# GNN on one core: first columns of edges counted beside the second table's zeroing, and the lower triangle in f32

## The chip, the cores and the metric

The kernel runs on one core of a Trainium2 chip. The metric is the device time of one execution, in microseconds. The median of three runs of the kernel before is 6590.73 us (6584.82 to 6592.37).

## The reference

Four graph layers follow each other on 3125 nodes with 96 features and 103125 directed edges (50000 random pairs in both directions, and one loop per node):

```
x = LN(x + GAT(x, edges))        # 3 layers, 4 heads: softmax over each node's edges
x = LN(x + GIN(x, src, dst))     # segment_sum(x[src], dst), then an MLP with batch norm
x = LN(x + dot_attention(x))     # softmax over edges of q[src].k[dst]
x = LN(x + edge_MLP(x, edge_attr_32))
```

An edge can occur more than once. The first three layers need for each pair of nodes only how often the pair is an edge. So the kernel counts the edges into a dense table of 3200 x 3200 cells once, and computes the layers densely from it.

## The kernel before, in words

`program` (line 101) calls `begin`, then `make_tables`, three attention layers, the other layers, and a store. Each part is a block of instructions per engine, and the next part starts when the last engine has finished the one before. The change is all in `begin` (line 175), the first stage.

`begin` does several things side by side. SyncE (SP) loads the inputs, and then issues the writes that zero the two halves of the count table in device memory (lines 241 to 245): two u16 tables `counts[0]` and `counts[1]` of 3200 x 3200 cells, each zeroed by 16 transfers from a tile of zeros, a row of 10,000 bytes from every partition, and by one small transfer of two bytes per partition, for 128 spare cells. All of these raise one semaphore, `zeroed`. Behind them on the same queue go 52 transfers that clear the table of sorted edges (line 250), whose rows are 16 x 34 x 4 = 2176 bytes a partition. TensorE and ScalarE project the first attention layer.

The edges lie in 806 columns of 128 (`ET` = 806), in 62 groups of `G` = 13 columns. For each group VectorE's `count(g)` (lines 385 to 406) finds, in every column, the edges that name the same cell. TensorE copies each column's cell numbers along the free axis into PSUM (line 331). VectorE compares them with the column itself into `same` (line 390), waits until the adds of the group before last have landed (lines 396 and 397), because `cell_slot` and `cell_add` have two halves only, sums `same` (398), casts the sums to `cell_add` (399), multiplies `same` by the lower triangle `earlier` (400), sums again (401), and so finds which edge is the first of its cell. The others are sent to a spare cell (402 to 405). Then `slots_ready` rises. `same` and `earlier` are bf16.

GpSimd (POOL) adds the counts into the table, one column with one indirect DMA (line 315, the "add" from here on): 128 read-modify-writes of two bytes each in device memory. It reads `cell_slot` and `cell_add`, which VectorE wrote. Two adds into one table may not be in flight together, since one that reads a cell before the other has written it would lose a count. So column t goes into table t % 2 and waits until the add before it in that table, t - 2, has landed. Before column 0 POOL waits for `zeroed`, 16 x 2 x 17, that is for both tables (line 308). At the end it waits for the last adds (line 318), and the block ends.

Beside the groups VectorE and TensorE find where each edge belongs in the sorted order: `members` after group 5 (line 417 is its long comparison), a histogram, and `place` after groups 16 to 36 (lines 455 to 460).

Of the kernel before, what the change touches and what calls it, by code (L numbers as in the profile page):

```python
# [19 lines left out]
P = 128  # L20
NT = -(-N // P)
NP = NT * P
NFULL = N // P
NREST = N - NFULL * P
ET = -(-E // P)
EREST = E - (P - 1) * ET
G = 13
# [30 lines left out]
f32, bf16, i32, u16 = mybir.dt.float32, mybir.dt.bfloat16, mybir.dt.int32, mybir.dt.uint16  # L58
ALU = mybir.AluOpType
# [4 lines left out]
def bcast_rows(ap, n):  # L64

    return ap.unsqueeze(0).to_broadcast([n, ap.shape[0]])
# [34 lines left out]
def program(nc, a, out):  # L101
    ctx = ExitStack()
    with ctx:
# [14 lines left out]
        with ExitStack() as c2:  # L118
# [14 lines left out]
            def project_first(xT, block, entry):  # L133
# [7 lines left out]
                return psum_free  # L141

            begin(nc, a, x, ident, wext, arow, counts, edges, project_first)
            make_tables(nc, a, ident, halves_rows, log_counts, edges)

# [22 lines left out]
def load_gat_weights(sp, a, layer, wext, arow, loaded):  # L168

    sp.dma_start(wext[:, 0:D], a["L0_gnn_W"][layer]).then_inc(loaded, 16)  # L170
    for k, name in enumerate(("L0_gnn_att_src", "L0_gnn_att_dst")):
        sp.dma_start(arow[:, k, :], bcast_rows(a[name][layer].rearrange("h c -> (h c)"), D)).then_inc(loaded, 16)


def begin(nc, a, x, ident, wext, arow, counts, edges, project):
# [6 lines left out]
    with ctx:  # L182
        ctx.enter_context(nc.cleanup_on_exit())
        sb = lambda n, s, d=f32: ctx.enter_context(nc.sbuf_tensor("pl" + n, s, d))
        sem = lambda n: nc.alloc_semaphore("st" + n)
        zeros = sb("zeros", [P, ZF], u16)
# [1 line left out]
        src_i, dst_i, block_i, local_i, part_i = (sb(n, [P, ET], i32) for n in ("src_i", "dst_i", "block_i", "local_i", "part_i"))  # L188
        cell, block_f, slot_f = (sb(n, [P, ET]) for n in ("cell", "block_f", "slot_f"))
        ends = sb("ends", [P, ET, 2])  # L190
        earlier, before, ones = (sb(n, [P, P], bf16) for n in ("earlier", "before", "ones"))
        xT = sb("xT", [D, NP])

        cell_slot = sb("cell_slot", [P, 2, G], i32)
        cell_add = sb("cell_add", [P, 2, G], u16)
# [18 lines left out]

        zeros_set, padded, x_padded, loaded, const_made, consts_ready, steps, row_cleared, row_made, rows_cleared = (
            sem(n) for n in ("zeros_set", "padded", "x_padded", "loaded", "const_made", "consts_ready", "steps", "row_cleared", "row_made", "rows_cleared"))
        zeroed = sem("zeroed")
        cells_made, slots_ready, rows_ready, rows_free = (sem(n) for n in ("cells_made", "slots_ready", "rows_ready", "rows_free"))
        added = [sem(f"added{w}") for w in range(2)]
        members_made, counted, hist_kept, summed, base_made, base_stored, rank_ready, rank_used, slots_made, stored = (  # L220
# [3 lines left out]
        HALF_T = RANK_T // 2  # L224
        LOADS = 11
        ZEROS = NP * NP // (P * ZF)
        with nc.Block() as block:
            @block.sync
            def _(sp):
                load_gat_weights(sp, a, 0, wext, arow, loaded)  # L230
                sp.wait_ge(x_padded, 1)
                sp.dma_start(x[:, 0:NFULL, :], a["x"][0:NFULL * P, :].rearrange("(t p) d -> p t d", p=P)).then_inc(loaded, 16)
                sp.dma_start(x[0:NREST, NFULL, :], a["x"][NFULL * P:N, :]).then_inc(loaded, 16)

                sp.wait_ge(padded, 2)
                for ap, t in ((a["src"], src_i), (a["dst"], dst_i)):
                    for lo, hi in ((0, 112), (112, P - 1)):
                        sp.dma_start(t[lo:hi, :], ap[lo * ET:hi * ET].rearrange("(p t) -> p t", t=ET)).then_inc(loaded, 16)
                    sp.dma_start(t[P - 1:P, 0:EREST], ap[(P - 1) * ET:E].rearrange("(p t) -> p t", p=1)).then_inc(loaded, 16)
                sp.wait_ge(zeros_set, 1)  # L240
                for part in counts:
                    v = part[0:NP * NP, :].rearrange("(p j f) o -> j p (f o)", p=P, f=ZF)
                    for j in range(ZEROS):
                        sp.dma_start(v[j], zeros[:]).then_inc(zeroed, 16)
                    sp.dma_start(part[NP * NP:NP * NP + P, :], zeros[:, 0:1]).then_inc(zeroed, 16)

                sp.wait_ge(row_made, 1)
                sorted_groups = edges["sorted"][:, :].rearrange("(g p k) w -> g p (k w)", p=P, k=TB)
                for g in range(SORTED_GROUPS):
                    sp.dma_start(sorted_groups[g], unused_row[:].rearrange("p k w -> p (k w)")).then_inc(rows_cleared, 16)  # L250

                sp.wait_ge(base_made, 1)
                sp.dma_start(edges["base"][:, :].rearrange("(c p) b -> p c b", p=P), base[:]).then_inc(base_stored, 16)
                sp.wait_ge(base_stored, 16)
                for n, (t, m) in enumerate(pieces):
                    if n >= 2:
                        sp.wait_ge(rank_used, n - 1)
                    sp.dma_start(base_row[:, n % 2, 0:m, :].rearrange("p t b -> p (t b)"),
                                 bcast_rows(edges["base"][t:t + m, :].rearrange("t b -> (t b)"), P)).then_inc(row_loaded[n % 2], 16)
                sp.wait_ge(base_made, 2)  # L260
                sp.dma_start(edges["column"][:, :].rearrange("(p c) o -> p (c o)", p=P), column_i[:]).then_inc(stored, 16)
                sp.wait_ge(slots_made, 1)
                sp.dma_start(edges["ends"][:, :, :], ends[:]).then_inc(stored, 16)
                sp.dma_start(edges["slot"][:, :], block_i[:]).then_inc(stored, 16)
                sp.wait_ge(stored, 48)
                sp.wait_ge(rows_cleared, 16 * SORTED_GROUPS)
# [38 lines left out]

            @block.gpsimd
            def _(pool):
                pool.wait_ge(zeroed, 16 * len(counts) * (ZEROS + 1))
                for t in range(ET):
                    g, j = divmod(t, G)  # L310
                    if j == 0:
                        pool.wait_ge(slots_ready, g + 1)
                    if t >= 2:
                        pool.wait_ge(added[t % 2], 16 * (t // 2))
                    nc.gpsimd.indirect_dma_start(counts[t % 2][:, :], bass.IndirectOffsetOnAxis(ap=cell_slot[:, g % 2, j:j + 1], axis=0),  # L315
                                                 cell_add[:, g % 2, j:j + 1], None, compute_op=ALU.add).then_inc(added[t % 2], 16)
                for w in range(2):
                    pool.wait_ge(added[w], 16 * (ET // 2))

            @block.tensor  # L320
            def _(pe):
# [53 lines left out]
            def _(dve):  # L375
# [9 lines left out]
                def count(g):  # L385

                    half = g % 2
                    key = cell[:, g * G:(g + 1) * G]
                    dve.wait_ge(rows_ready, g + 1)
                    nc.vector.tensor_tensor(same[:], rows[:, 0:G * P].rearrange("p (t c) -> p t c", c=P),  # L390
                                            key.unsqueeze(2).to_broadcast([P, G, P]), ALU.is_equal).then_inc(rows_free, 1)
                    dve.wait_ge(rows_free, g + 1)
                    if g >= 2:

                        done = (g - 1) * G
                        dve.wait_ge(added[0], 16 * -(-done // 2))
                        dve.wait_ge(added[1], 16 * (done // 2))
                    step(nc.vector.reduce_sum(nlow[:], same[:], axis=AX.X))  # L398
                    step(nc.vector.tensor_copy(cell_add[:, half, :], nlow[:]))
                    step(nc.vector.tensor_tensor(same[:], same[:], earlier[:].unsqueeze(1).to_broadcast([P, G, P]), ALU.mult))  # L400
                    step(nc.vector.reduce_sum(nlow[:], same[:], axis=AX.X))
                    step(nc.vector.tensor_scalar(first[:], nlow[:], 0.0, None, ALU.is_equal))
                    step(nc.vector.tensor_scalar(moved[:], key, spare[:, 0:1], None, ALU.subtract))
                    step(nc.vector.tensor_tensor(moved[:], moved[:], first[:], ALU.mult))
                    step(nc.vector.tensor_scalar(cell_slot[:, half, :], moved[:], spare[:, 0:1], None, ALU.add))
                    dve.sem_inc(slots_ready, 1)
# [1298 lines left out]
```

## Time and profile before

| | us |
|---|---|
| median of 3 runs | 6590.73 |
| lowest, highest | 6584.82, 6592.37 |
| the profiled execution, first to last instruction | 6972.0 |
| add (line 315), 806 of them, busy | 1310.8 |
| idle of POOL just before them | 430.7 |
| first and last start of an add | 138.0, 1742.7 |

For the profiled execution nothing but this span is given. "Busy" is the time in which an engine worked on instructions; "idle before" is the time between the end of its previous instruction and the start of this one, with the one who ended most of it. Of an add the time is that which POOL takes to make its descriptors, not the transfer, which lands later.

### The profile page before, as it was taken

To read this page: it belongs to the slowest core of one execution; us is meant where nothing else is said; L and a number is where in the kernel's file an instruction comes from. 1 tells how busy PE (TensorE), PEld (TensorE's weight loads), DVE (VectorE), ACT (ScalarE), POOL (GpSimd) and SP (SyncE) were. 2 spreads that over 40 slices of the span, in tenths; PEclk is the share of its full clock that TensorE was granted. 3 is DMA by queue.
4 is the path that set the end of the run, shared out by engine and by line. 5 is a ranking of instruction groups with operands and counts; after the bars stand their busy time and mean duration, and the time that the engine had idled before them with its cause. 6 is when DMAs were issued, how large, how long until landed. Compare 5 with 4: busy or idle time off the path is not lost. (4 is left out here: it accounts for less than half of the span.)

```text
span 6972.0 us, 62328 instructions
## 1 busy us (share of the span) xinstructions
PE 3698.9 (53%) x21452; PEld 2183.6 (31%) x21452; DVE 3889.8 (56%) x4318; ACT 2472.8 (35%) x4050; POOL 4020.6 (58%) x3151
## 2 busy tenths in 40 slices
PE   2111111110428888477784878876888454555444
PEld 1111011110424444244442444443333232333232
DVE  1434443332679996599965999654999521121113
ACT  1000000000327777377773777721666311111111
POOL 1888878888607667076670666701860256655652
PEclk6555555555668898698985889877888666665656
DMA  9222222222979987398962898752222111111111
GB/s 330 1 7 18 18 18 7 0 0 0 327 235 209 205 208 149 88 212 200 209 147 78 206 208 206 157 181 90 82 77 72 32 39 41 43 41 40 41 39 24
DMA packets 410083, 747.21 MB, mean 107 GB/s; under 512 B 173421, under 2 KB 251291, under 8 KB 405678
## 3 DMA queue, kind: packets, MB, share of 16 engines
q0 software_dynamic: 237024, 305.69, 28.3%
q1 hardware_dynamic: 169534, 436.30, 18.7%
q8 instruction: 178, 2.92, 0.2%
q10 hardware_dynamic: 3216, 1.23, 0.1%
q14 instruction: 131, 1.07, 0.0%
HBM read 628.59 MB, written 114.40 MB: 107 GB/s over the span
## 5 line engine op out<-in xcount | busy, mean ns | idle before, releaser
L315 POOL DMA_INDIRECT counts<-plcell_add,plcell_slot x806 | 1310.8, 1626 | 430.7 <-issue 236.9
L1574 POOL DMA_INDIRECT emxg<-xtab,emsrc x832 | 804.7, 967 | 555.5 <-DVE emsrc L1616 299.6
L398 DVE TENSOR_REDUCE plnlow<-plsame 128x13 f32<-128x1664 bf16 x62 | 117.0, 1888 | 1032.7 <-DMA counts<-plcell_add,plcell_slot 1032.6
L331 PE MATMUL plrows<-ident,plcell 128*128 128x128 f32 x806 | 186.0, 421 | 943.6 <-DVE plsame L390 942.9
L1659 PE MATMUL emps_m<-emwe,emfeatT 128*128 128x384 f32 x416 | 280.6, 769 | 682.4 <-issue 367.1
L652 ACT ACT_TABLE_LOAD x1 | 1.3, 1283 | 1706.5 <-PE mtps L640 1706.5
L1626 DVE TENSOR_TENSOR emsame<-emlocal_id,emrow 128x512 f32<-128x512 f32 x208 | 144.4, 694 | 694.8 <-DMA plbase_row<-slot_base 495.8
L1086 PE MATMUL ga1psE<-ident,ga1logit 128*128 128x128 f32 x2500 | 404.0, 301 | 228.8 <-DMA ga1logit<-log_counts 146.4
L1086 PE MATMUL ga2psE<-ident,ga2logit 128*128 128x128 f32 x2500 | 405.6, 303 | 222.1 <-DMA ga2logit<-log_counts 145.8
L1086 PE MATMUL ga0psE<-ident,ga0logit 128*128 128x128 f32 x2500 | 406.9, 303 | 219.1 <-DMA ga0logit<-log_counts 151.4
L1598 ACT ACTIVATE emfeatT<-emps_f 128x128 f32<-128x128 f32 x208 | 57.8, 278 | 1199.6 <-remote 740.0
L331 PEld LDWEIGHTS plrows<-ident,plcell 128*128 128x128 f32 x806 | 161.4, 224 | 976.8 <-DVE plsame L390 975.9
L1040 ACT ACTIVATE ga1prob<-ga1psE,ga1src_fifth 128x512 f32<-128x512 f32 (+1 forms) x700 | 405.4, 667 | 153.6 <-PE ga1psE L1086 130.5
L1040 ACT ACTIVATE ga2prob<-ga2psE,ga2src_fifth 128x512 f32<-128x512 f32 (+1 forms) x700 | 405.0, 665 | 152.0 <-PE ga2psE L1086 123.6
L1040 ACT ACTIVATE ga0prob<-ga0psE,ga0src_fifth 128x512 f32<-128x512 f32 (+1 forms) x700 | 405.6, 669 | 139.4 <-PE ga0psE L1086 124.9
L1086 PEld LDWEIGHTS ga2psE<-ident,ga2logit 128*128 128x128 f32 x2500 | 293.7, 151 | 448.1 <-issue 265.1
L1086 PEld LDWEIGHTS ga0psE<-ident,ga0logit 128*128 128x128 f32 x2500 | 293.8, 151 | 447.0 <-issue 252.9
L1086 PEld LDWEIGHTS ga1psE<-ident,ga1logit 128*128 128x128 f32 x2500 | 291.3, 150 | 453.0 <-issue 280.2
L1668 PE MATMUL emps_a<-emmsg,emsame 128*128 128x96 f32 x1664 | 387.5, 375 | 22.8 <-DVE emsame L1626 8.5
L1668 PEld LDWEIGHTS emps_a<-emmsg,emsame 128*128 128x128 f32 x1664 | 338.0, 271 | 196.0 <-issue 195.1
L1470 ACT ACTIVATE dotwork<-dotpsS 128x640 f32<-128x640 f32 x500 | 313.1, 708 | 205.9 <-PE dotpsS L1418 204.5
L1502 DVE TENSOR_TENSOR dotwork<-dotwork,dotcnt 128x1280 f32<-128x1280 f32 x250 | 374.8, 1499 | 8.6
(339 smaller groups left out, 9058.8 us busy)
## 6 DMA issues: line engine op xcount, KB each, us to landing
ga0logit<-log_counts POOLq DMA_DIRECT2D x96, 512.0 KB
ga1logit<-log_counts POOLq DMA_DIRECT2D x96, 512.0 KB
ga2logit<-log_counts POOLq DMA_DIRECT2D x96, 512.0 KB
counts<-plzeros SPq DMA_DIRECT2D x32, 1250.0 KB
mthalf<-counts SPq DMA_DIRECT2D x50, 800.0 KB
log_counts<-mtlogs SPq DMA_DIRECT2D x25, 1600.0 KB
ga0near<-log_counts SPq DMA_DIRECT2D x50, 800.0 KB
ga1near<-log_counts SPq DMA_DIRECT2D x50, 800.0 KB
```

The lines of the kernel that those rows point to most:

```text
L315: nc.gpsimd.indirect_dma_start(counts[t % 2][:, :], bass.IndirectOffsetOnAxis(ap=cell_slot[:, g % 2, j:j + 1], axis=0), cell_add[:, g % 2, ...
L331: last = nc.tensor.transpose(rows[:, j * P:(j + 1) * P], cell[:, g * G + j:g * G + j + 1].to_broadcast([P, P]), ident[:])
L398: step(nc.vector.reduce_sum(nlow[:], same[:], axis=AX.X))
L1040: nc.scalar.activation(prob[:, u % P_BUFS, 0:width], psE[:, u % E_BUFS, 0:width], ACT.Exp, bias=src_fifth[:, tile(r, t), h:h + 1]).then_in ...
L1086: last = nc.tensor.transpose(psE[:, u % E_BUFS, q * P:(q + 1) * P], logit[:, r % L_BUFS, q, t * P:(t + 1) * P], ident[:])
L1470: nc.scalar.activation(work[:, t % W_BUFS, 2 * g:2 * g + 2, f * HW:(f + 1) * HW], psS[:, n % S_BUFS, :, 0:HW], ACT.Exp).then_inc(exp_ready, 1)
L1502: nc.vector.tensor_tensor(w, w, cnt[:, t % C_BUFS, cols].unsqueeze(1).to_broadcast([P, HEADS, HW]), ALU.mult).then_inc(prob_ready, 1)
L1574: nc.gpsimd.indirect_dma_start(xg[:, h, t, :], None, xtab[:, :], bass.IndirectOffsetOnAxis(ap=src[:, h, t:t + 1], axis=0)).then_inc(gather ...
L1598: nc.scalar.activation(featT[:, v % 2, :], ps_f[:, 0:P], ACT.Copy).then_inc(feat_kept, 1)
L1626: nc.vector.tensor_tensor(same[:, v % 2, :, :], local_id[:].unsqueeze(1).to_broadcast([P, CT, P]), row[:, g % ROWS, lo:lo + CT, ED:ED + 1] ...
L1659: nc.tensor.matmul(ps_m[:, v % 2, 0:CT * D], featT[:, v % 2, :], we[:].rearrange("p t d -> p (t d)"), start=True, stop=True).then_inc(pre_ ...
L1668: last = nc.tensor.matmul(flat_a[:, bass.ds(lo, D)], same[:, w % 2, t, :], msg[:, w % 2, t, :], start=False, stop=(w == CHUNKS - 1 and t = ...
```

## The change

Each table gets its own semaphore, `zeroed[0]` and `zeroed[1]`. POOL waits for the one at the first add into its table. The first 16 columns (`LONE`) all go into table 0, each waiting for the one before; column 16 is the first of table 1, and from there columns alternate. `table_of(t)` gives the table and how many adds it has had; `adds_before(t, w)` counts those of the columns before t, for VectorE's wait and for the one at the end. `earlier` becomes f32; `same` stays bf16.

```diff
-        earlier, before, ones = (sb(n, [P, P], bf16) for n in ("earlier", "before", "ones"))
+        earlier = sb("earlier", [P, P])
+        before, ones = (sb(n, [P, P], bf16) for n in ("before", "ones"))
...
-        zeroed = sem("zeroed")
+        zeroed = [sem(f"zeroed{w}") for w in range(2)]
...
+        LONE = 16
+
+        def table_of(t):
+
+            return (0, t) if t < LONE else ((t - LONE + 1) % 2, LONE + (t - LONE) // 2 if (t - LONE) % 2 else (t - LONE) // 2)
+
+        def adds_before(t, w):
+
+            return sum(table_of(u)[0] == w for u in range(t))
...
-                for part in counts:
+                for part, done in zip(counts, zeroed):
...
-                        sp.dma_start(v[j], zeros[:]).then_inc(zeroed, 16)
-                    sp.dma_start(part[NP * NP:NP * NP + P, :], zeros[:, 0:1]).then_inc(zeroed, 16)
+                        sp.dma_start(v[j], zeros[:]).then_inc(done, 16)
+                    sp.dma_start(part[NP * NP:NP * NP + P, :], zeros[:, 0:1]).then_inc(done, 16)
...
-                pool.wait_ge(zeroed, 16 * len(counts) * (ZEROS + 1))
                 for t in range(ET):
                     g, j = divmod(t, G)
+                    w, n = table_of(t)
                     if j == 0:
                         pool.wait_ge(slots_ready, g + 1)
-                    if t >= 2:
-                        pool.wait_ge(added[t % 2], 16 * (t // 2))
-                    nc.gpsimd.indirect_dma_start(counts[t % 2][:, :], bass.IndirectOffsetOnAxis(ap=cell_slot[:, g % 2, j:j + 1], axis=0),
-                                                 cell_add[:, g % 2, j:j + 1], None, compute_op=ALU.add).then_inc(added[t % 2], 16)
+                    if n == 0:
+                        pool.wait_ge(zeroed[w], 16 * (ZEROS + 1))
+                    else:
+                        pool.wait_ge(added[w], 16 * n)
+                    nc.gpsimd.indirect_dma_start(counts[w][:, :], bass.IndirectOffsetOnAxis(ap=cell_slot[:, g % 2, j:j + 1], axis=0),
+                                                 cell_add[:, g % 2, j:j + 1], None, compute_op=ALU.add).then_inc(added[w], 16)
                 for w in range(2):
-                    pool.wait_ge(added[w], 16 * (ET // 2))
+                    pool.wait_ge(added[w], 16 * adds_before(ET, w))
...
-                        done = (g - 1) * G
-                        dve.wait_ge(added[0], 16 * -(-done // 2))
-                        dve.wait_ge(added[1], 16 * (done // 2))
+                        for w in range(2):
+                            if adds_before((g - 1) * G, w):
+                                dve.wait_ge(added[w], 16 * adds_before((g - 1) * G, w))
```

## Rows read from the trace of the kernel before

**Rows 1.** The page, 40 slices of the span: busy tenths of POOL.
```profile
POOL 1888878888607667076670666701860256655652
```

**Rows 2.** The page's groups: busy, mean ns | idle before and who ended it.
```profile
L315 POOL DMA_INDIRECT counts<-plcell_add,plcell_slot x806 | 1310.8, 1626 | 430.7 <-issue 236.9
...
L398 DVE TENSOR_REDUCE plnlow<-plsame 128x13 f32<-128x1664 bf16 x62 | 117.0, 1888 | 1032.7 <-DMA counts<-plcell_add,plcell_slot 1032.6
```

**Rows 3.** Line 315: durations in ns (min/median/max), first and last start in us.
```profile
L315 POOL DMA_INDIRECT counts<-plcell_add,plcell_slot x806: 1557/1561/21401, 138.0 to 1742.7; - x162
```

**Rows 4.** Timeline, group 2: start us, us, instruction [idle before <-releaser].
```profile
180.05 1.89 DVE L398 TENSOR_REDUCE plnlow<-plsame 128x13 f32<-128x1664 bf16 x1 [104.99 <-DMA counts<-plcell_add,plcell_slot]
...
182.19 1.02 DVE L400 TENSOR_TENSOR plsame<-plsame,plearlier 128x1664 bf16<-128x1664 bf16 x1
182.47 2.18 POOL L315 DMA_INDIRECT counts<-plcell_add,plcell_slot  x1 [0.30 <-issue]
...
184.95 1.56 POOL L315 DMA_INDIRECT counts<-plcell_add,plcell_slot  x1 [0.30 <-issue]
```

**Rows 5.** Timeline, group 61, the last.
```profile
1698.90 1.02 DVE L400 TENSOR_TENSOR plsame<-plsame,plearlier 128x1664 bf16<-128x1664 bf16 x1
1699.12 2.24 POOL L315 DMA_INDIRECT counts<-plcell_add,plcell_slot  x1 [0.30 <-issue]
```

**Rows 6.** Timeline, `members` after group 5.
```profile
265.06 21.15 DVE L417 TENSOR_TENSOR plmember<-plblock_f,plblock_id 128x20150 bf16<-128x20150 f32 x1
266.23 21.40 POOL L315 DMA_INDIRECT counts<-plcell_add,plcell_slot  x1 [0.30 <-issue]
```

**Rows 7.** Timeline, a much later stage, gathers beside a comparison in f32.
```profile
5614.95 0.69 DVE L1626 TENSOR_TENSOR emsame<-emlocal_id,emrow 128x512 f32<-128x512 f32 x1 [0.22 <-PE emps_a L1668]
5615.00 1.46 POOL L1574 DMA_INDIRECT emxg<-xtab,emsrc  x1 [3.48 <-DVE emsrc L1616]
5616.76 0.95 POOL L1574 DMA_INDIRECT emxg<-xtab,emsrc  x1 [0.31 <-issue]
```

**Rows 8.** Timeline, the first comparison of group 3, one operand in PSUM.
```profile
186.24 1.89 DVE L390 TENSOR_TENSOR plsame<-plrows,plcell 128x1664 bf16<-128x1664 f32 x1
186.82 1.56 POOL L315 DMA_INDIRECT counts<-plcell_add,plcell_slot  x1 [0.30 <-issue]
```

**Rows 9.** Groups by line and form, DVE, 150 to 1744 us: busy, mean ns | idle.
```profile
L390 DVE TENSOR_TENSOR plsame<-plrows,plcell 128x1664 bf16<-128x1664 f32 x59 | 111.5, 1891 | 5.7
L400 DVE TENSOR_TENSOR plsame<-plsame,plearlier 128x1664 bf16<-128x1664 bf16 x60 | 61.5, 1025 | 2.1
...
L459 DVE TENSOR_TENSOR plranked<-plranked,plmember 128x1000 f32<-128x1000 f32 x20 | 24.0, 1200 | 0.7
```

**Rows 10.** Timeline of DVE: the slots of group 1 are ready.
```profile
72.79 0.23 DVE L405 TENSOR_SCALAR plcell_slot<-plmoved,plspare 128x13 int32<-128x13 f32 x1
```

**Rows 11.** Timeline of SP's DMA queue: start us, us that the issue took.
```profile
60.77 15.71 SPq L244 DMA_DIRECT2D counts<-plzeros  x1
...
98.26 68.04 SPq L250 DMA_DIRECT2D sorted_edges<-plunused_row  x52
```

**Rows 12.** Three stretches: length, busy of five engines, PEclk, DMA share, GB/s.
```profile
20.00:60.00 40.00, 36.40 (x128) 22.27 (x127) 10.44 (x38) 15.00 (x28) 0.00 (x0) 0.83 1.01 421
60.00:65.00 5.00, 1.23 (x6) 0.82 (x4) 4.68 (x8) 0.00 (x0) 0.00 (x0) 0.50 1.66 118
120.00:125.00 5.00, 0.00 (x0) 0.00 (x0) 0.00 (x0) 0.00 (x0) 0.00 (x0) 0.50 1.73 217
```

**Rows 13.** Timeline of POOL: adds 0, 4, 6 and 12.
```profile
137.97 1.79 POOL L315 DMA_INDIRECT counts<-plcell_add,plcell_slot  x1 [135.18 <-DMA counts<-plzeros]
...
151.77 1.56 POOL L315 DMA_INDIRECT counts<-plcell_add,plcell_slot  x1 [3.15 <-DMA counts<-plcell_add,plcell_slot]
...
158.62 1.56 POOL L315 DMA_INDIRECT counts<-plcell_add,plcell_slot  x1 [3.18 <-DMA counts<-plcell_add,plcell_slot]
...
176.88 1.56 POOL L315 DMA_INDIRECT counts<-plcell_add,plcell_slot  x1 [1.12 <-DMA counts<-plcell_add,plcell_slot]
```

## The prediction, made before the changed kernel was run

> **What bounds the kernel now.** I read the slices first. POOL is nearly idle in the first slice and at 70 to 80% in the next nine, which is the first stage [rows 1]. The groups say with what: 806 adds, busy for 1310.8 us, with 430.7 us idle before them, of which 236.9 is issue, that is POOL's own 0.30 us between two adds [rows 2]. VectorE waits in that stage: before line 398 it idles 1032.7 us in total, until adds land [rows 2]; less the 105.0 us of group 2 [rows 4] that is 15.7 us for each of the 59 groups behind it. So POOL's chain of adds, from 138.0 to 1742.7 us [rows 3], is the stage, and the later stages start when it is done. What lengthens one add, or moves the first, moves the end; VectorE has some 15 us a group to spare. The pace is 1.56 + 0.30 = 1.86 us an add.
>
> The timeline then shows that adds are not all alike. In group 2 one add takes 2.18 us in place of 1.56; it starts 0.28 us after VectorE began line 400, and ends 1.44 us after line 400's end, where 1.56 less about 0.12 would put an add that had stood still until then [rows 4]. In the last group it is the same: 2.24 us, started 0.22 us in [rows 5]. Following the timeline, each of the 60 groups between has one add that starts in line 400's 1.02 us, 0.22 to 0.79 us after its start. The totals confirm it: 1310.8 less 806 x 1.561 [rows 3] is 52.6 us; one long add took 21.40 - 1.56 = 19.8 of it [rows 6]; 32.8 us is left, or 0.55 us in each of 60 groups.
>
> **The triangle in f32.** Two questions: how long is line 400 then, and does an add still stand still behind it.
>
> Duration. Line 400 has bf16 throughout and takes 1.025 us. Line 390 has as many elements with f32 among its inputs and takes 1.891 us; line 459 multiplies f32 by bf16, 1000 elements, in 1.200 us, the same rate for its size [rows 9]. So I take 1.89 us, 0.866 us more. Bounds: 0 (1.025 us stays) and 0.87.
>
> The standing still. It does with f32 inputs and at the slow rate: line 417 runs 21.15 us, an add that starts 1.17 us into it takes 21.40 us, so it resumed when line 417 was over [rows 6]. It does with f32 inputs and an f32 output: line 1626 runs 0.69 us, a gather that starts 0.05 us into it takes 1.46 us, the next 0.95 [rows 7]. What does not do it is one SBUF operand: line 390, with one operand in PSUM, runs for 1.89 us and the add that starts inside takes 1.56 [rows 8]. So it is not the bf16 rate that holds POOL, but two operands in SBUF, and line 400 keeps both there. The add that starts 0.3 us in will stand until 1.89 instead of 1.02. The next one would start after that, so one add a group is hit as now.
>
> Cost: 60 x 0.866 = 52.0 us, all on POOL's chain, which has no slack inside a group. Bounds: if in an execution without the profiler the adds fall otherwise against line 400, the added stall of a group is anything from 0 (no start in the longer window) to 0.87; 0 and 52 us. I take 52, since the only trace there is shows the hit in all 60 groups. VectorE's own chain grows by 0.87 us a group, under those 15.7 us.
>
> The Trainium skill ("SBUF — State Buffer", Who interferes with whom) says that a VectorE instruction with two SBUF inputs contends with a GpSimd instruction that reads SBUF, whatever the mode; the trace agrees, 19.8 us in [rows 6] and none in [rows 8]. The same section infers that a tensor_tensor should leave descriptor generation alone, as it takes only the read side; by that the whole term would be nothing, and [rows 4, 6] speak against it, the index columns being read from SBUF.
>
> **The first adds.** The slots of groups 0 and 1 are ready at 73.0 us [rows 10]. When is table 0 zeroed? The rate drops from 421 GB/s to a mean of 118 in 60 to 65 us and 217 in 120 to 125 [rows 12]: it stops at 60 + 5 x 118/421 = 61.4 us and at 122.6 us, where each table's bulk is out and its small transfer waits for it. After the second stop, POOL goes 15.4 us later, at 137.97 [rows 13]. SP's issue of a transfer at 60.77 is held for 15.71 us, to 76.5 [rows 11]. Both give 76.5 to 76.8 us for table 0. The first add starts at 76.8, 61.2 us sooner.
>
> Each of the 16 must then land before the next starts. Undisturbed, add 12 starts at 176.88 and VectorE, which waits for it, goes at 180.05 [rows 13, 4]: 3.2 us from one to the next. Beside the clearing of sorted edges it is 158.62 - 151.77 = 6.85 us [rows 13]. Beside the zeroing no row shows it. Bounds: 3.2 us, and an add that does not land before 138. The pieces there are 10,000 bytes against 2,176, and the small transfer needed 15.4 us to land behind such pieces. The extra 3.65 us behind small pieces, times 4.6, would make 20 us an add; I take the 15.4 that was seen.
>
> Now: 61.2/15.4 = 4.0 adds by 138; to 177, where clearing ends, 39/6.85 = 5.7 more; the other 6.3 at 3.2 us take 20 us. Add 16 starts at 197; before, at 184.95 [rows 4]. So this part costs 12 us: before, the twelve adds up to 176.88 went two in flight, one in each table, and this order gives that up exactly where landing is slow. At the ends: with 3.2 us all 16 are done by 128, add 16 waits for table 1 until 138, and from there everything runs as before but 16 adds ahead, 16 x 1.86 = 30 us gained. With none done by 138, 5.7 come by 177 and 10.3 x 3.2 = 33 us more, 210 us, a loss of 25. With the clearing's 6.85 us it would be a gain of 4.
>
> The Trainium skill ("DMA: Bandwidth & Descriptors", Queues, rings and completion order) says that a completion increment lands only after every earlier write of that DMA engine, across its queues; the wait of 15.4 us in [rows 12, 13] agrees. By this rule an add beside the zeroing waits for the zero pieces in front of it.
>
> **At nothing.** One more wait at column 16 (both adds and zeroes done by then); the f32 memset and select of `earlier`, before 3 us, under POOL's idle 135 us; queue order of SP's transfers, unchanged; the counts of the two tables, whose sum alone is used later. Group 2's slots need 13 landed adds, and 13 more adds of group 1 cover them.
>
> **Sum.** Against the profiled execution: 6972.0 + 52 + 12 = 7036 us. The runs' median lies 381 us below its span, and I can't say in which stage; I carry the difference over as it is: 6590.7 + 64 = 6655 us.
>
> **Rivals.** (a) The f32 triangle frees POOL: line 400 leaves the fast bf16 rate and with it whatever held the adds. This ends on the other side: the 0.55 us of each group goes, 60 x 0.55 = 33 us gained, and with the loss of 12 the time is 6570 us; it decides wherever one add starts inside line 400. For it: the only bf16 product is the one that stalls adds in every group. Against it: [rows 6, 7], which are clear. 3%.
>
> (b) The early adds do overlap the zeroing: they land in 3.2 us, 30 us are gained, 6590.7 + 52 - 30 = 6613 us. For it: an add moves 128 x 2 bytes. Against: 6.85 us behind much smaller pieces. 15%.
>
> (c) The stall does not grow by all of 0.87 us a group, since without the profiler adds and line 400 stand otherwise: halfway, 26 us, 6590.7 + 26 + 12 = 6629 us; at its end, 6603. For it: the profiled execution is 5.8% longer, so something in it is slower. Against: adds and line 400 are tied, VectorE starting on the landing of an add. 15%.
>
> (d) The adds also hold up the zeroing behind them, as the small transfer did for 15.4 us: with three such stops table 1 and the clearing are 46 us late, and the lone adds stay slow longer: 6590.7 + 52 + 12 + 46 = 6701 us at most. Against: POOL's adds between 138 and 177 went beside the clearing with no stop of that length. 5%.
>
> The forecast has 62%, its own range 6635 to 6668 us (the stall at 45 to 52, the start at 0 to 25). The range reaches down to (b) and (c): 6605 to 6675. No change that a measurement can tell is within 0.2%, 13 us: 6577.5 to 6604; there lie the far end of (c) and (b) with part of (c), 6%. Faster has (a) and (b) with all of (c), 5%. Slower 89%.
>
> **What would show it.** Line 400 at 1.89 us, and one add a group near 3.0 us (2.18 + 0.87); the adds' mean at 1.69 us, 1363 us busy. If those adds are at 1.56 us, (a) is right. First add near 77 us; gaps of about 13 us between the next few, and add 16 near 197 us. If add 16 stands at 138 us, (b) is right. The last add near 1807 us; everything behind it shifted and otherwise as it was. Wrong would be a line 400 at 1.02 us, or a stage that ends with other than POOL.

## The result, and the profile after

The changed kernel takes 6638.31 us (median of four runs; 6632.37 to 6639.27), the kernel before on the same chip 6587.77 us (also four runs). The ratio is 1.008, with a 95% interval of 1.0067 to 1.0092: 50.5 us slower, where 64 us were forecast, and the time lies inside the range.

Start with the adds on POOL. These are the page's groups and the view of line 328 (the old 315) of the changed kernel; the columns are those of [rows 2, 3]. The lone line behind them is that of the kernel before.

```profile
L328 POOL DMA_INDIRECT counts<-plcell_add,plcell_slot x806 | 1360.0, 1687 | 433.8 <-issue 235.1
...
L411 DVE TENSOR_REDUCE plnlow<-plsame 128x13 f32<-128x1664 bf16 x62 | 117.0, 1888 | 1035.6 <-DMA counts<-plcell_add,plcell_slot 1035.6
```

```profile
L328 POOL DMA_INDIRECT counts<-plcell_add,plcell_slot x806: 1557/1562/21399, 78.4 to 1795.1; - x162
its engine sat idle before it (us, times) until:
  issue: 235.1, 761
  DMA counts<-plcell_add,plcell_slot: 123.2, 44
  DMA counts<-plzeros: 75.6, 1
```

```profile
  DMA counts<-plcell_add,plcell_slot: 58.6, 40
```

The last add starts at 1795.1 us; before, at 1742.7 [rows 3]. The 52.4 us split into two parts: the adds are busy 1360.0 - 1310.8 = 49.2 us longer, and POOL idles 433.8 - 430.7 = 3.1 us longer before them [rows 2]. The first add is 59.6 us sooner, but the waits for landings grow from 58.6 to 123.2 us, which takes all of it back.

Next, where the 49 us are. The groups of VectorE (150 to 1800 us, columns as in [rows 9]), and the timeline of groups 3 and 61, answering to [rows 4, 5]:

```profile
L413 DVE TENSOR_TENSOR plsame<-plsame,plearlier 128x1664 bf16<-128x1664 bf16 x60 | 113.5, 1892 | 2.1
```

```profile
213.25 1.89 DVE L413 TENSOR_TENSOR plsame<-plsame,plearlier 128x1664 bf16<-128x1664 bf16 x1
213.71 2.86 POOL L328 DMA_INDIRECT counts<-plcell_add,plcell_slot  x1 [0.30 <-issue]
...
1750.31 1.89 DVE L413 TENSOR_TENSOR plsame<-plsame,plearlier 128x1664 bf16<-128x1664 bf16 x1
1750.83 2.81 POOL L328 DMA_INDIRECT counts<-plcell_add,plcell_slot  x1 [0.30 <-issue]
```

The multiply takes 1.892 us in place of 1.025. (The view names the first input's type, bf16; the triangle's f32 doesn't show in it, the duration does.) In each of the 59 groups from 3 on one add starts inside it, 0.21 to 0.98 us after its start, and ends 1.4 us after its end; most take 3.0 us where they took 2.16. VectorE's idle time before line 411 is 1035.6 us, against 1032.7 [rows 2]: the longer multiply takes nothing from VectorE's spare time, and the stage is longer because POOL's adds are.

Last, the start of the stage, answering to [rows 13]. The timeline of POOL: adds 0, 1, 4, 5, 6, then 15 and 16.

```profile
78.35 1.79 POOL L328 DMA_INDIRECT counts<-plcell_add,plcell_slot  x1 [75.57 <-DMA counts<-plzeros]
87.31 1.59 POOL L328 DMA_INDIRECT counts<-plcell_add,plcell_slot  x1 [7.17 <-DMA counts<-plcell_add,plcell_slot]
...
114.66 1.56 POOL L328 DMA_INDIRECT counts<-plcell_add,plcell_slot  x1 [7.64 <-DMA counts<-plcell_add,plcell_slot]
125.69 1.56 POOL L328 DMA_INDIRECT counts<-plcell_add,plcell_slot  x1 [9.47 <-DMA counts<-plcell_add,plcell_slot]
141.93 1.56 POOL L328 DMA_INDIRECT counts<-plcell_add,plcell_slot  x1 [14.68 <-DMA counts<-plcell_add,plcell_slot]
...
189.38 1.56 POOL L328 DMA_INDIRECT counts<-plcell_add,plcell_slot  x1 [1.82 <-DMA counts<-plcell_add,plcell_slot]
191.25 1.56 POOL L328 DMA_INDIRECT counts<-plcell_add,plcell_slot  x1 [0.30 <-issue]
```

Beside the zeroing one lone add follows the other after 9.0 us, and add 5, whose landing meets the stretch in which table 1's small transfer is under way, takes 16.2 us. Add 16 starts at 191.25; before, at 184.95 [rows 4]. The early start bought nothing: add 16 is 6.3 us behind.

The profiled execution spans 6636.3 us, while that of before spanned 6972.0 for a kernel that runs in 6588. The edit doesn't explain that difference: GpSimd's first transfer of the second stage still starts 52 us later than before (1802.3 against 1750.0), while the edge layer's gathers ran from 5515.1 to 6862.7 us before and from 5502.4 to 6546.4 us after, 304 us less, with nothing edited there. So only the first stage is compared between those two traces.

### The profile page after: what moved, and what is told of

The parts are those of the page before. It is cut to its first block and busy times, and to the rows that moved or that the text cites. A ratio compares the mean times of both kernels' runs of the same rounds, so it can differ in the third digit from the quotient of the medians.

```text
span 6636.3 us, 62328 instructions
## 1 busy us (share of the span) xinstructions
PE 3847.1 (58%) x21452; PEld 2266.4 (34%) x21452; DVE 3921.9 (59%) x4318; ACT 2493.0 (38%) x4050; POOL 4053.6 (61%) x3151
## 5 line engine op out<-in xcount | busy, mean ns | idle before, releaser
L328 POOL DMA_INDIRECT counts<-plcell_add,plcell_slot x806 | 1360.0, 1687 | 433.8 <-issue 235.1
L411 DVE TENSOR_REDUCE plnlow<-plsame 128x13 f32<-128x1664 bf16 x62 | 117.0, 1888 | 1035.6 <-DMA counts<-plcell_add,plcell_slot 1035.6
L1643 DVE TENSOR_TENSOR emmsg<-emps_m,emxg 128x384 f32<-128x384 f32 x208 | 115.9, 557 | 812.4 <-DMA emxg<-xtab,emsrc 791.8
L1681 PE MATMUL emps_a<-emmsg,emsame 128*128 128x96 f32 x1664 | 455.8, 453 | 147.9 <-DVE emsame L1639 135.2
L1681 PEld LDWEIGHTS emps_a<-emmsg,emsame 128*128 128x128 f32 x1664 | 404.5, 311 | 381.7 <-issue 377.9
L1672 PE MATMUL emps_m<-emwe,emfeatT 128*128 128x384 f32 x416 | 340.2, 921 | 76.2 <-ACT emfeatT L1611 76.2
L941 DVE CUSTOM_DVE_ANT_0 ga1unused<-ga1near,src_row 128x1600 bf16<-128x1600 f32 x200 | 366.2, 1831 | 8.2 <-DMA ga1near<-log_counts 6.0
```

The costliest lines, as they stand in the source:

```text
L328: nc.gpsimd.indirect_dma_start(counts[w][:, :], bass.IndirectOffsetOnAxis(ap=cell_slot[:, g % 2, j:j + 1], axis=0), cell_add[:, g % 2, j:j ...
L941: nc.vector.tensor_tensor_reduce(out=unused[:], in0=near[:, f, :], in1=src_row[:, h, f * HALF:(f + 1) * HALF], scale=1.0, scalar=LOWEST, o ...
L1643: nc.vector.tensor_tensor(msg[:, v % 2, :, :].rearrange("p t d -> p (t d)"), ps_m[:, v % 2, 0:CT * D], xg[:, g % 2, lo:lo + CT, :].rearran ...
L1672: nc.tensor.matmul(ps_m[:, v % 2, 0:CT * D], featT[:, v % 2, :], we[:].rearrange("p t d -> p (t d)"), start=True, stop=True).then_inc(pre_ ...
L1681: last = nc.tensor.matmul(flat_a[:, bass.ds(lo, D)], same[:, w % 2, t, :], msg[:, w % 2, t, :], start=False, stop=(w == CHUNKS - 1 and t = ...
```

## Experiments

The first four ran beside 21 runs of the kernel before (median 6583.86 us), the last four beside another 21 (6594.10 us). A difference in us is one of medians; the ratio, with its 95% interval, is worked out from all runs, and the two can differ by some 3 us.

**The triangle alone.** Lines of the kernel before, with this edit:

```diff
-        earlier, before, ones = (sb(n, [P, P], bf16) for n in ("earlier", "before", "ones"))
+        earlier = sb("earlier", [P, P])
+        before, ones = (sb(n, [P, P], bf16) for n in ("before", "ones"))
```

> The kernel before with the lower triangle in f32 and nothing else. Theory (two SBUF operands hold POOL for as long as the VectorE instruction runs): line 400 takes 1.89 us, one add a group takes about 3.0 us instead of 2.15, 60 x 0.85 = 51 us more. Rival 1 (the f32 triangle costs little and the 50 us came from the first adds): within 10 us of before. Rival 2 (only the bf16 rate holds POOL): 33 us less than before.

Measured: 6635.38 us, ratio 1.0077 (1.0063 to 1.0090), 51.5 us slower. The page's row of the adds:

```profile
L316 POOL DMA_INDIRECT counts<-plcell_add,plcell_slot x806 | 1363.1, 1691 | 431.3 <-issue 237.0
```

Busy 52.3 us longer, idle as before. This is the theory's number, in runs and in the trace, and both rivals fall. The triangle alone costs as much as the whole change did in its first measurement.

**The lone columns alone.** The changed kernel with the first edit above taken back.

> The changed kernel with the triangle back in bf16: the first 16 columns go into table 0 alone. Theory: add 16 starts 6 us later than in the kernel before, as in the changed kernel, so 6 us more than before (0 to 12). Rival 1 (the first adds made the 50 us): 50 us more. Rival 2 (the overlap does gain what it was to gain, and the triangle hid it): 20 to 30 us less.

Measured: 6592.59 us, ratio 1.0010 (1.0001 to 1.0019), 8.7 us more. Both rivals fall: neither 50 us more nor 20 to 30 less is near it. The adds' row: busy as before, idle 8.9 us longer.

```profile
L327 POOL DMA_INDIRECT counts<-plcell_add,plcell_slot x806 | 1309.9, 1625 | 439.6 <-issue 234.8
```

**The f32 triangle, read from PSUM.** TensorE copies it once with the identity; the prefix sums move into the histogram's bank, so that a bank is free. The f32 lines of the first experiment belong to this edit too; they, the new semaphore and VectorE's one wait for it are left out here.

```diff
-            psB = ctx.enter_context(nc.psum_tensor("plpsB", [P, 512], f32))
+            psE = ctx.enter_context(nc.psum_tensor("plpsE", [P, 512], f32))
+            psB = psH[:, 256:512]
...
                 psum_free(pe)
+                nc.tensor.matmul(psE[:, 0:P], ident[:], earlier[:], start=True, stop=True).then_inc(triangle_made, 1)
...
-                    step(nc.vector.tensor_tensor(same[:], same[:], earlier[:].unsqueeze(1).to_broadcast([P, G, P]), ALU.mult))
+                    step(nc.vector.tensor_tensor(same[:], same[:], psE[:, 0:P].unsqueeze(1).to_broadcast([P, G, P]), ALU.mult))
```

> The kernel before with the triangle in f32, copied once by TensorE into a PSUM bank of its own and read from there by line 400 (the prefix sums share the histogram's bank). The multiply still runs at the slow rate, but has one SBUF operand. Theory (two SBUF operands hold POOL): line 400 at 1.9 us, no add stretched by it, so the 0.55 us of each group goes too: 33 us less than before. Rival (a longer line 400 holds POOL longer, wherever its operands lie): 50 us more, as with the f32 triangle in SBUF.

Measured: 6549.20 us, ratio 0.9943 (0.9929 to 0.9957), 34.7 us less than before. The adds' row on the page, the multiply's group, and the timeline of group 2:

```profile
L318 POOL DMA_INDIRECT counts<-plcell_add,plcell_slot x806 | 1278.0, 1586 | 428.9 <-issue 235.0
```

```profile
L405 DVE TENSOR_TENSOR plsame<-plsame,plpsE 128x1664 bf16<-128x1664 bf16 x60 | 113.3, 1888 | 2.1
```

```profile
184.02 1.89 DVE L405 TENSOR_TENSOR plsame<-plsame,plpsE 128x1664 bf16<-128x1664 bf16 x1
184.32 1.56 POOL L318 DMA_INDIRECT counts<-plcell_add,plcell_slot  x1 [0.31 <-issue]
...
186.19 1.56 POOL L318 DMA_INDIRECT counts<-plcell_add,plcell_slot  x1 [0.30 <-issue]
```

The multiply is as long as with the f32 triangle in SBUF, the add again starts 0.30 us into it, and it takes its 1.56 us; so it is in all 60 groups. So neither the length nor the number format holds POOL, but the second operand in SBUF. Between this run and the first experiment lie 86 us, and what differs is where one operand lies, with the bookkeeping that this needs. By which part of the machine a second SBUF operand holds POOL, no run here shows.

**Six lone columns.** The changed kernel with the bf16 triangle and `LONE = 6`.

> As the kernel with 16 lone columns and the triangle in bf16, but with 6 lone columns. In the changed kernel an add beside the zeroing landed after 9.0 us, so 6 are in by the time table 1 is zeroed; from there the columns alternate at once, two in flight. Theory (the lone order is what loses, beside the clearing of the sorted edges): adds run 5 to 6 ahead of before, 5.5 x 1.86 = 10 us less than before, and 16 us less than with 16 lone columns. Rival (any early add costs as much as it gains, since it slows the zeroing): no change from before.

Measured: 6572.42 us, ratio 0.9982 (0.9973 to 0.9991), 11.4 us less than before and 20.2 less than with 16. Adds 5, 6 and 7 on POOL's timeline:

```profile
127.05 1.56 POOL L327 DMA_INDIRECT counts<-plcell_add,plcell_slot  x1 [10.84 <-DMA counts<-plcell_add,plcell_slot]
139.69 1.56 POOL L327 DMA_INDIRECT counts<-plcell_add,plcell_slot  x1 [11.08 <-DMA counts<-plzeros]
142.09 1.56 POOL L327 DMA_INDIRECT counts<-plcell_add,plcell_slot  x1 [0.84 <-DMA counts<-plcell_add,plcell_slot]
```

Five adds are in when table 1 is zeroed, and the sixth lands about when add 7, which waits for it, starts at 142.09. Add 6 starts the moment table 1 is ready, and from there two are in flight. The last add starts at 1728.8 us, 13.9 us sooner than before [rows 3]. The rival, no change, falls. The idea of counting early was sound; sixteen columns were too many, and six pay (numbers between weren't tried).

**The clearing later.** The kernel before, with one wait ahead of the clearing of the sorted edges:

```diff
                 sp.wait_ge(row_made, 1)
+                sp.wait_ge(slots_ready, 6)
```

> The kernel before, but SP clears the sorted edges only after the slots of group 5 are ready, at about 260 us, where one add stands still behind line 417 for 20 us anyway. Theory (the first 12 adds take 39 us instead of 22 because they land beside the clearing): adds run at 1.86 us from the first one, 15 us less there; some 11 us of the clearing outlast the standstill and cost 5, so 10 us less than before. Rival (the slow landings at the start are due to the zeroing's last writes, or the cost only moves along with the clearing): no change from before.

Measured: 6575.25 us, ratio 0.9976 (0.9966 to 0.9986), 18.9 us less by the medians and 16 (9 to 22) by the ratio; in the trace the last add is 12.2 us sooner than in [rows 3]. The rival falls; whether it is more than the expected 10 us, the runs can't tell. The first adds (0, 1, 2) show why:

```profile
137.62 1.79 POOL L316 DMA_INDIRECT counts<-plcell_add,plcell_slot  x1 [134.84 <-DMA counts<-plzeros]
139.71 1.59 POOL L316 DMA_INDIRECT counts<-plcell_add,plcell_slot  x1 [0.30 <-issue]
141.60 1.56 POOL L316 DMA_INDIRECT counts<-plcell_add,plcell_slot  x1 [0.30 <-issue]
```

From add 1 on they go at 1.87 us each, with no wait for a landing. Add 12 starts at 160.24 in place of 176.88 [rows 13], 16.6 us sooner. Some 6 us are lost again in group 4: the clearing moves data from about 246 to 284 us, POOL stands still from 250.5 to 271.0, and the adds behind that wait for landings again.

**Zeroing in small pieces.** 16 lone columns, bf16 triangle, `ZF = 1250`.

> 16 lone columns and the triangle in bf16, with zeroing in pieces of 2500 bytes a partition instead of 10,000 (64 transfers a table instead of 16). Theory (an add beside the zeroing waits for pieces in front of it, so its landing time goes with their size): 9.1 us from one lone add to the next becomes about 7 us, as beside the clearing with its pieces of 2176 bytes; add 16 starts some 6 us earlier than with large pieces. Rival (it waits for a fixed backlog of bytes, or for device memory): 9 us as before.

Measured: 6604.53 us, ratio 1.0020 (1.0011 to 1.0029), 10.4 us more. Lone adds 2 to 6:

```profile
99.38 1.56 POOL L327 DMA_INDIRECT counts<-plcell_add,plcell_slot  x1 [5.80 <-DMA counts<-plcell_add,plcell_slot]
107.17 1.56 POOL L327 DMA_INDIRECT counts<-plcell_add,plcell_slot  x1 [6.24 <-DMA counts<-plcell_add,plcell_slot]
115.86 1.56 POOL L327 DMA_INDIRECT counts<-plcell_add,plcell_slot  x1 [7.13 <-DMA counts<-plcell_add,plcell_slot]
123.42 1.56 POOL L327 DMA_INDIRECT counts<-plcell_add,plcell_slot  x1 [6.00 <-DMA counts<-plcell_add,plcell_slot]
131.08 1.56 POOL L327 DMA_INDIRECT counts<-plcell_add,plcell_slot  x1 [6.11 <-DMA counts<-plcell_add,plcell_slot]
```

From 84.38 to 131.08 us there are six steps of 7.8 us, against 9.0 with pieces four times as large. The rival, 9 us as before, falls, but four times smaller pieces take off only an eighth. If the wait beyond the 3.2 us of an undisturbed add has one part that goes with the size and one that doesn't, 4.6 us here and 5.8 there make the second part some 4.2 us. That is an estimate, since the zeroing's rate changed too, and what the second part waits for stays open. And the small pieces don't pay. The stretches of this kernel (columns as in [rows 12]) show that small pieces move slower:

```profile
20.00:60.00 40.00, 30.31 (x123) 17.50 (x122) 16.67 (x46) 15.00 (x28) 0.00 (x0) 0.98 1.04 373
...
80.00:120.00 40.00, 0.00 (x0) 0.00 (x0) 0.00 (x0) 0.00 (x0) 8.05 (x5) 0.50 1.04 348
```

373 GB/s against 421 [rows 12], and beside the lone adds 348 against 418 in the changed kernel. Table 0 is zeroed 6 us later, and add 16 starts at 198.99 us, 5 us later than with large pieces (193.99). My expectation of 6 us sooner was wrong for this reason.

**What helped, together.** 6 lone columns, the triangle in PSUM, the clearing after group 5.

> All that helped together: 6 lone columns, the triangle read from PSUM, the clearing after group 5. With the triangle in PSUM 35 us less, with 6 lone columns 11 us less, with the later clearing 10 us less than before, if they add up: 56 us less, about 6530 us. Rival (the later clearing and the 6 lone columns save the same wait beside the clearing, and don't add up): about 6540 us.

Measured: 6533.56 us, ratio 0.9909 (0.9895 to 0.9923), 60.5 us less than before and 116 less than the changed kernel beside it. By medians the parts, 34.7 + 11.4 + 18.9, are 65; by the start of the last add they are 34.6 + 13.8 + 12.2 = 60.6, and here it is 57.5 us sooner. So they add up, within what the runs can tell (51 to 69 us), and the rival's 6540 us, which is 46 us less, lies outside.

```profile
L331 POOL DMA_INDIRECT counts<-plcell_add,plcell_slot x806 | 1278.8, 1587 | 405.2 <-issue 235.7
```

Busy 32.0 us and idle 25.5 us less than in [rows 2].

**The change again.**

> The changed kernel once more, beside the same runs of the kernel before as its parts. If the two parts add up, 52 + 9 = 60 us more than before. If they interact, the 50 us of the first measurement: with lone adds the add that starts 1.8 us into line 400 of group 2 escapes the stall, which can explain 1.5 us and no more.

Measured: 6649.40 us, ratio 1.0087 (1.0073 to 1.0101), 55.3 us more. With the first measurement of 50.5 that is 53 us; the parts make 60. The intervals of about 9 us to either side allow both. The trace says more. The adds' row, and adds 5 and 6 on POOL's timeline:

```profile
L328 POOL DMA_INDIRECT counts<-plcell_add,plcell_slot x806 | 1361.4, 1689 | 438.4 <-issue 235.3
```

```profile
123.87 1.56 POOL L328 DMA_INDIRECT counts<-plcell_add,plcell_slot  x1 [7.56 <-DMA counts<-plcell_add,plcell_slot]
145.13 1.56 POOL L328 DMA_INDIRECT counts<-plcell_add,plcell_slot  x1 [19.70 <-DMA counts<-plcell_add,plcell_slot]
```

The adds are busy 50.6 us longer than before and POOL idles 7.7 us longer before them, 58.3 together. The two traces of one kernel thus differ by 6 us, and half of that is how long the adds at the second small transfer take to land: adds 4 and 5 take 30.4 us together here, 21.3 of it add 5, and 27.3 in the first trace, and add 16 is 9.6 us behind in place of 6.3. The traces of the two parts add up to 61 us, 3 more than here and 9 more than in the first trace. About 1 us is the add that escaped; the remaining few can't be told from such differences.

## Why the prediction came out as it did

*What bounds.* Right. What the last add moved, the end moved: in seven of the eight experiments the two agree within about 3 us, and with the clearing later they are 12.2 and 18.9 (16 by the ratio). VectorE's longer multiply by itself cost nothing: read from PSUM it is as long, and the kernel is faster than before.

*The triangle in f32.* Right by mechanism and nearly by size. Duration: 1.89 forecast, 1.892 measured. Standing still: one add a group, as forecast, in 59 groups where I counted 60. In group 2 the lone order had moved the adds: none starts until 1.79 us into the multiply, and it isn't stretched. The term was 52.0 us; the adds' busy time grew by 49.2 and 50.6 in the two traces of the changed kernel, and by 52.3 with the triangle alone. That two SBUF operands are what holds POOL was read from [rows 6 to 8] and is now shown by the triangle in PSUM. Rival (a), that f32 frees POOL, falls with its sign; rival (c) falls too: the runs without a profile moved by what the profiled stall says, 51.5 us. Its one support, the long profiled execution, lay elsewhere: 304 us of it in the edge layer.

*The first adds.* Table 0 was zeroed at 78.35 us (forecast 76.8), and the loss had the forecast's sign, but the term was sized at 12 us and measured 6.3 and 9.6 at add 16 in the two traces of the changed kernel, 9.0 in the trace of it alone (8.7 in those runs). The step that was off is the price of a lone add beside the zeroing. I took the 15.4 us that the small transfer had needed, and 4.0 adds; it is 9.0 us, and 5 land before 126 with a sixth at 142. The 15.4 us belong to that transfer's own stretch, in which hardly any data moves: only the adds that met it paid such a price, the last of them 16.2 us (20.5 and 21.3 in the two later traces with 16 lone columns). Nor is this stretch a wait for zero pieces still being written in front, as I read it: the last section has it with the engines idle. Scaling the clearing's wait by the size of the pieces would have been worse, 20 us, and the small pieces speak against scaling: four times smaller, they took off 1.2 us. The rest went as forecast, 6.8 us an add beside the clearing and 3.3 alone.

*Rivals (b) and (d).* (b), adds that land in 3.2 us, is refuted by 9.0. (d), adds that hold up the zeroing, did not show: table 1 was ready at 136.65 and 139.69 us in the two kernels with six lone adds, and at 137.6 to 140.5 in the four traces without any ([rows 13] is one); the zeroing kept 418 GB/s beside the lone adds, against 421. With 16 lone columns that moment isn't seen, since add 16 comes later.

The sum, 64 us, was 9 to 14 us too large by the two measurements. In the traces the lone adds account for 2 to 6 us of that and the stall for 1 to 3; the rest is within what the runs can tell.

## What to carry to other kernels

When GpSimd issues the DMAs on the critical path, look at which VectorE instruction runs as each starts, and where that one's operands lie. With two in SBUF, the issue of an indirect DMA waited here for that instruction's end, and a slower number format made the wait longer; an operand moved to PSUM ended it, though the instruction stayed at 1.89 us. Work started early beside a bulk transfer is worth as much of it as lands there: give up the two in flight for about that many columns, not for more.

## What was not expected of the hardware

While each table's small transfer (128 pieces of two bytes behind 20 MB) was under way, the DMA engines moved next to nothing for some 15 us. These are three stretches of the changed kernel, columns as in [rows 12]:

```profile
110.00:115.00 5.00, 0.00 (x0) 0.00 (x0) 0.00 (x0) 0.00 (x0) 0.34 (x1) 0.50 1.05 414
...
125.00:130.00 5.00, 0.00 (x0) 0.00 (x0) 0.00 (x0) 0.00 (x0) 1.56 (x1) 0.50 1.03 31
130.00:135.00 5.00, 0.00 (x0) 0.00 (x0) 0.00 (x0) 0.00 (x0) 0.00 (x0) 0.50 0.98 68
```

The engines count as busy (1.03) at 31 GB/s; here the clearing is queued behind. With the clearing later nothing stands behind table 1's small transfer in SyncE's queue, and these are two stretches of the kernel with all that helped, and its add 6, which waits for that table:

```profile
125.00:130.00 5.00, 0.00 (x0) 0.00 (x0) 0.00 (x0) 0.00 (x0) 0.00 (x0) 0.50 0.20 6
130.00:135.00 5.00, 0.00 (x0) 0.00 (x0) 0.00 (x0) 0.00 (x0) 0.00 (x0) 0.50 0.00 0
```

```profile
136.65 1.56 POOL L331 DMA_INDIRECT counts<-plcell_add,plcell_slot  x1 [12.09 <-DMA counts<-plzeros]
```

The bulk is out at about 123 us and the engines are idle from 130, yet table 1 counts as zeroed only at 136.6 (137.6 in the kernel with the clearing alone moved). So the wait is as long with nothing moving, and data still being moved, in front or behind, isn't what makes it; what does stays open. The stretch comes once per table in the traces of all these kernels; what it would bring to zero the spare cells in another way wasn't tried.

The hold works in the other direction too, for a short instruction. With the triangle in PSUM the two engines' work fell otherwise against each other, and VectorE's line 410 (the old 405; it reads one SBUF tile and a column of scalars) took 0.44 us on average in place of 0.23, while adds were being issued:

```profile
L410 DVE TENSOR_SCALAR plcell_slot<-plmoved,plspare 128x13 int32<-128x13 f32 x60 | 26.5, 441 | 2.1
```

The timeline shows when. Where line 410 starts 0.25 to 0.38 us after an add, it takes 0.23 us; where it starts 0.48 to 0.59 us after one, in 43 groups, it takes 0.45 to 0.56 and ends 1.03 to 1.05 us after the add's start each time. Before, it always started 0.9 us after an add and took 0.23.
